# Two masked attentions: the low halves of the fourth step move from GpSimd to VectorE

## The reference, cut to what matters

```python
# first layer (attention a): cosine scores
att = softmax(where(adj > 0, Kn @ Qn.T, NEG), axis=1)
prop = att @ features
...
# third layer (attention b): scaled scores
scores = where(adj > 0, q @ k.T / sqrt(d), neg)
out = elu(softmax(scores, axis=-1) @ v)
```

## Time and profile before

| | us |
|---|---|
| median of 3 runs | 1434.35 |
| lowest and highest run | 1434.26, 1439.12 |
| the profiled execution | 1429.9 |
| its span, first to last instruction | 1428.1 |
| busy in the span: PE, PEld, DVE, ACT, POOL | 1294.5, 793.7, 1280.7, 1131.4, 841.3 |
| mean granted TensorE clock | 0.974 of full speed |

### The profile page before, as it was taken

The page is one execution under the profiler, slowest core; times in us unless marked ns, Lnnn a source line. Parts: engine busy times, 40 slices in busy tenths (PEclk is TensorE's granted clock), DMA queues, the critical chain, the costliest instruction groups (busy, mean ns, idle before and its releaser), DMA issues. The chain is left out here.

```text
span 1428.1 us, 27595 instructions
## 1 busy us (share of the span) xinstructions
PE 1294.5 (91%) x7723; PEld 793.7 (56%) x7723; DVE 1280.7 (90%) x2230; ACT 1131.4 (79%) x1774; POOL 841.3 (59%) x1071
## 2 busy tenths in 40 slices
PE   5699999999985999999999996999999999899895
PEld 4444444444434888888888884344444444333664
DVE  7699999999997999999999998789999999966753
ACT  5677777676765999999999996787888778767773
POOL 4264665666658999999999996123323333216554
PEclk9899999999997999999999998999999999999997
DMA  7054555554528993000000000455555555204330
GB/s 263 1 203 180 187 196 177 176 202 180 182 83 294 334 330 120 0 0 0 0 0 0 0 0 1 148 199 184 193 190 197 188 200 182 84 2 144 95 91 24
DMA packets 65798, 186.76 MB, mean 131 GB/s; under 512 B 4515, under 2 KB 47539, under 8 KB 49234
## 3 DMA queue, kind: packets, MB, share of 16 engines
q1 hardware_dynamic: 62738, 179.74, 37.0%
q0 software_dynamic: 3008, 6.37, 1.3%
HBM read 145.51 MB, written 41.49 MB: 131 GB/s over the span
## 5 line engine op out<-in xcount | busy, mean ns | idle before, releaser
L1060 PEld LDWEIGHTS r_p_y<-w_ffn,r_z_t 128*128 128x128 f32 x1920 | 255.7, 194 | 6.7
L1060 PE MATMUL r_p_y<-w_ffn,r_z_t 128*128 128x128 f32 x1920 | 255.6, 277 | 0.0
L1271 POOL TENSOR_TENSOR r_stat<-r_stat,minus_half 128x4 f32<-128x4 f32 x240 | 244.2, 1018 | 18.8
L831 POOL TENSOR_TENSOR b_lo<-b_prob,b_hi 128x1024 f16<-128x1024 f32 x32 | 80.0, 2499 | 251.7 <-ACT b_hi L800 251.7
L897 DVE SCALAR_TENSOR_TENSOR b_prob<-adj_rows,b_prob 128x1024 f32<-128x1024 int32 x128 | 188.1, 1473 | 25.5 <-ACT b_prob L793 25.2
L897 DVE SCALAR_TENSOR_TENSOR a_prob<-adj_rows,a_prob 128x1024 f32<-128x1024 int32 x128 | 192.3, 1506 | 13.5 <-ACT a_prob L793 13.5
L793 ACT ACTIVATE b_prob<-b_p_s,shift,g_unit 128x1024 f32<-128x1024 f32 x128 | 154.0, 1203 | 53.0 <-PE b_p_s L722 52.8
L793 ACT ACTIVATE a_prob<-a_p_s 128x1024 f32<-128x1024 f32 x128 | 130.9, 1023 | 70.4 <-PE a_p_s L722 70.4
L1196 DVE BATCH_NORM_STATS2 r_parts<-r_z 128x6 f32<-128x256 f32 x480 | 182.1, 421 | 0.0
L831 POOL TENSOR_TENSOR a_lo<-a_prob,a_hi 128x1024 f16<-128x1024 f32 x32 | 87.4, 2730 | 144.1 <-ACT a_hi L800 144.1
L1189 DVE SCALAR_TENSOR_TENSOR r_h<-r_tanh,r_p_y 128x512 f32<-128x512 f32 x232 | 158.8, 684 | 3.6 <-ACT r_tanh L1128 0.9
(11 more groups left out here) (289 smaller groups left out, 3023.0 us busy)
## 6 DMA issues: line engine op xcount, KB each, us to landing
adj_rows<-in_adj_t SPq DMA_DIRECT2D x128, 1024.0 KB, 4.8
sorted_rows<-blank SPq DMA_DIRECT2D x7, 4160.0 KB
x_got<-sorted_rows SPq DMA_DIRECT2D x46, 130.0 KB
sorted_rows<-blank SPq DMA_DIRECT2D x1, 4290.0 KB
x_rows<-in_x SPq DMA_DIRECT2D x4, 512.0 KB, 8.7
wd_raw<-in_wd SPq DMA_DIRECT2D x1, 2048.0 KB, 10.0
late<-in_late SPq DMA_DIRECT2D x1, 756.0 KB
out_x<-b_rows,x_to_row POOLq DMA_INDIRECT x46
```

What stands on the lines that cost most here:

```text
L831: nc.gpsimd.tensor_tensor(lo[POOL_STEP][:], prob[POOL_STEP][:], hi[POOL_STEP][:], ALU.subtract).then_inc(s["lo_pool_ready"], 1)
L1060: last = nc.tensor.matmul(out[:, D * t:D * t + D], z_t[g % R][:, P * t:P * t + P], k.w_ffn[:], start=False, stop=(t == TPC - 1), skip_grou ...
L1271: nc.gpsimd.tensor_tensor(stat[g][:, 1, :], stat[g][:, 0, :], k.minus_half[:], ALU.pow)\
```

## The change

Every low half is made by DVE: `lows` on DVE no longer leaves out step 3, POOL's `lows` is gone, and with it the constant `POOL_STEP` and the semaphore `lo_pool_ready`. `lo_ready` now counts four a quad, and everyone who waits for a low half waits on it.

```diff
-            if st == POOL_STEP:
-                eng.wait_ge(s["lo_pool_ready"], f + 1)
-            else:
-                eng.wait_ge(s["lo_ready"], 3 * f + st + 1)
+            eng.wait_ge(s["lo_ready"], 4 * f + st + 1)
...
         @block.gpsimd
         def _(pool):
-            def lows(f):
-                pool.wait_ge(s["hi_ready"], 4 * f + POOL_STEP + 1)
-                wait_used(pool, f, POOL_STEP)
-                nc.gpsimd.tensor_tensor(lo[POOL_STEP][:], prob[POOL_STEP][:], hi[POOL_STEP][:],
-                                        ALU.subtract).then_inc(s["lo_pool_ready"], 1)
-
...
                 for q in range(QUADS):
-                    lows(QUADS * c + q)
                     if is_a:
                         split_weights(c, q)
...
             def lows(f, st):
-                if st == POOL_STEP:
-                    return
                 dve.wait_ge(s["hi_ready"], 4 * f + st + 1)
```

More of the change, by code:

```diff
@@ L647, in attention @@
     LAG = 3
-    POOL_STEP = 3
     QUADS = STEPS // 4
@@ L663, in attention @@
         p_o = [k.ps(f"{tag}p_o{i}", [P, CHUNK], ctx) for i in range(2)]
-        names = ("s_ready", "exp_ready", "masked", "hi_ready", "lo_ready", "lo_pool_ready", "o_ready")
+        names = ("s_ready", "exp_ready", "masked", "hi_ready", "lo_ready", "o_ready")
         s = {n: k.sem(tag + n, ctx) for n in names}
```

## The result

| | before | after |
|---|---|---|
| median of 4 runs each (us) | 1435.92 | 1416.62 |
| lowest and highest run | 1434.26, 1439.12 | 1415.34, 1420.53 |
| the profiled execution, its span | 1429.9, 1428.1 | 1420.53, 1418.7 |
| length of a | 368.2 | 356.5 |
| length of b | 355.4 | 349.65 |

The ratio is **0.9867**, 95% interval 0.9839 to 0.9896: 1.3% shorter, which the interval sets apart from no change. The forecast was 1417.7 us, range 1403 to 1430. A second measurement, among the experiments, gave 0.9892 (0.9867 to 0.9916).

What follows compares the result with a forecast made beforehand. PE is the floor, and DVE, held up by POOL's low halves, keeps the kernel off it. Terms -8.4 (chunks of a), -5.6 (b), -2.6 (end of a) sum to -16.6: 1434.35 becomes 1417.7 us, range 1403 to 1430.

Steps and rivals of the forecast that it cites:

- PE's floor: Both attentions: PE needs 42.3 us a chunk and stands still for 3.1 in a, 1.4 in b.
- POOL's low halves are what makes DVE late: Both attentions: DVE loses 6.0 us a chunk in a and 4.7 in b to POOL's low halves.
- The rival that the lengthening is DVE's own: Both attentions: long masks not due to POOL, so added low halves cost in full; 1476 us, chance 0.08.
- b: Attention b: PE becomes the bound, about 0.5 us of standstill stays, chunk 43.72 to 42.9; -5.6 us for 7 chunks.
- A chunk of a: Attention a: DVE's need becomes 44.2 us, a chunk falls from 45.36 to about 44.2; -8.4 us for chunks 1 to 7.
- the term for the burst: Attention a: POOL's 12 unpaced pieces run together and cost DVE 1.3 us more a chunk, between 0 and 2.7.
- the rival in which the burst is paid in full: Attention a: POOL's pieces hold DVE for 5.2 us, chunks stay at 45.4; 1426 us, chance 0.22.
- DVE stays the bound: Attention a: DVE's need of 44.2 us a chunk stays above PE's 42.3 and sets the chunk's length.
- The end of a: Behind a's last chunk: `begin` starts earlier, DVE's copy is last, next block's first tanh comes sooner; -2.6 us.

Runs made afterwards that it cites:

- the two experiments with POOL's pieces out and in: Kernel before without POOL's low halves, none in their place: 1398.49 us; changed kernel with an unused POOL 128x1024 subtraction a quad in b: 1475.23 us.
- The memset in a: Changed kernel plus a one-column memset on DVE behind the mask of each odd step of attention a: 1428.57 us.

## Why the prediction was right, point by point

- **PE's floor and what lies over it.** Right: 42.33 us in both attentions once nothing holds PE.
- **POOL's low halves are what makes DVE late.** Right. In b masks and low halves had 188.1 + 116.5 - 224 x 1.21 = 33.6 us of lengthening, 4.2 a chunk where one chunk was read as 4.7; now (156.6 + 156.5 - 256 x 1.21) / 8 = 0.4. The rival that the lengthening is DVE's own falls by the two experiments with POOL's pieces out and in.
- **b.** Right in size and place: chunks of 42.86 for 42.9, 0.5 us of standstill left as foretold, -5.8 us for -5.6.
- **A chunk of a.** The mechanism was right, the term for the burst too large. The prediction had 2.5 + 1.3 = 3.8 us a chunk for POOL's other pieces; measured are 2.8 without (2.5 in masks and low halves, 0.4 in the small subtraction) and 3.1 with the burst, in which that subtraction is short, so the burst adds 0.3 to 0.6. A chunk fell by 1.5 us, not 1.2: 7 x 1.5 = 10.5 for 8.4. One reason the prediction didn't have: the piece ahead of the burst is held off, and the burst falls into the first steps of the next chunk. Where it ran right behind the statistics, as the prediction had it, a chunk without a turn of the loop took 45.05 us, near the 45.4 of the rival in which the burst is paid in full; the memset there changed more than the place, so this reason is argued, not shown.
- **"DVE stays the bound"** was too simple. With the same instructions on DVE (the memset apart), moved or beside POOL's pieces at other times, a chunk took 43.25, 43.86, 44.37 or 45.05 us. What holds PE is DVE being late at a few places, not the sum of its work.
- **The end of a: this step failed.** "With the change `begin` can start when the rows are measured, at 419.35, and is no longer last." It did start then (414.09, by after's clock), but its first piece took 6.79 us and the whole ended 1.18 us behind DVE's copy. The last chunk and what follows it gave some 0.8 us beyond the 1.5 of other chunks, not 2.6. The memset in a shows that the stay was the cause of 1.2 of the missing 1.8: without it the first tanh starts 1.00 us behind the copy's start in place of 2.20, as the prediction had it. The other 0.6 is the copy, which came 0.3 us earlier and not 0.95 (430.95 - 430.0); why stays open. This miss of 1.8 us and the 2.1 too little for the chunks nearly cancel; the total is better than its parts, and that is luck.
- Not foreseen: the stretch behind b, from the start of DVE's last copy of the sums to the last instruction, took 176.5 us before and 176.8 to 179.3 in the eleven traces with the changed order in b. With b as before it took 177.5, and 178.1 without POOL's low halves, so that the order in b isn't shown to be the cause.

## What to carry to other kernels

Before giving VectorE's work to GpSimd, subtract what the row beside it loses: here a 128x1024 piece on POOL took up to a piece's length from DVE, and taking 32 of them back in each attention paid some 17 us although DVE was busy for over 95% of a chunk. When a wait that paced an engine goes, its other work becomes a burst; look where it will fall, since with the same 12 pieces PE stood still for 1.51 us a chunk in one place and for 2.65 in another, the memset apart. A wait of their own that puts the split's pieces where DVE has room, with the finish spread, gave 5.9 us more in a. And an instruction that is put into a loop to probe something can cost more than itself: look at the turns of the loop before the difference is put down to what was probed.

## What the runs showed of the hardware that was not expected

- **A small GpSimd piece can wait for a long row of VectorE instructions, not for one.** 128x4, 0.20 us alone, stayed 11.33 us in a and 8.90 in b, beside masks and low halves that followed each other with no gap. The Trainium skill, "SBUF — State Buffer", section "SBUF: two separate sides", says that whichever of the two starts first has the port pair for that instruction, and the other blocks. The mask that POOL met at 326.21 was over at 327.4, and POOL still waited ten us more: the rows go beyond that rule. The stay in a ended at 337.70, at a pause of DVE of 0.16 us, the one in b at 1030.00, just after DVE's copy of the sums began. With a memset in DVE's stream the piece got in behind one mask, with no memset in between. Elsewhere too POOL gets in between adjacent instructions (its burst and DVE's rows of 2 us take turns from 300 to 309), so back-to-back instructions alone don't decide; what does is open.
- **PE's clock fell inside a stage that ran without a break.** After standstills of 3.20 us (in b, with POOL's added subtraction) and 3.53 us (in a, with the memset) the granted clock was 0.50, that is 1.2 GHz, over the next 2.5 and 5 us. In the run of the 3.53 it stayed at 1.00 behind a standstill of 3.52, so the length of the standstill alone doesn't decide. A late engine can so cost more than the wait.
- **A loop that grew loaded its code again.** With 64 memsets of 0.06 us in a, 8 a chunk, the queue of instructions moved 11 packets between 240 and 430 us where it moves none in the changed kernel, and DVE stood still for 1.4 to 2.3 us at a time at both turns of its loop, inputs done. In b, where the same memset gives a loop of 257 instructions, no such pause is seen. That the loads are DVE's is inferred from the times and from the loop being all that grew.
